# Moving the edge marks and the 0/1 test from the dense layers into the edge layer of a four-layer graph network

## The reference, cut to what matters

```python
x = _layernorm(x + L0(x, adj, nodemask))   # (1+eps) x + adj^T x, two-layer MLP, mask
x = _layernorm(x + L1(x, adj, adj))        # neighbour mean, projection, relu
x = _layernorm(x + L2(x, adj))             # normalised adjacency, projection
x = _layernorm(x + L3(x, adj))

def L3(x, adj):                            # the edge layer
    hi, hj = x @ W1[:H], x @ W1[H:]
    h = relu(hi[:, :, None, :] + hj[:, None, :, :] + b1)   # one row for each pair i, j
    y = layernorm(h @ W2 + b2) * gamma + beta
    return einsum('bij,bijh->bih', adj, y)
```

## Time and profile before

| | us |
|---|---|
| median of 3 runs | 467.81 (466.93 to 469.84) |
| the profiled execution's own time | 470.96 |
| its span, first to last instruction | 469.1 |
| TensorE busy | 439.8 (94%) |
| VectorE busy | 413.1 (88%) |
| ScalarE busy | 386.1 (82%) |
| GpSimd busy | 358.9 (76%) |

### The profile page before, as it was taken

The page is one execution under the profiler, slowest core; times in us unless marked ns, Lnnn a source line. Parts: engine busy times, 40 slices in busy tenths (PEclk is TensorE's granted clock), DMA queues, the critical chain, the costliest instruction groups (busy, mean ns, idle before and its releaser), DMA issues. The chain is left out here.

```text
span 469.1 us, 14149 instructions
## 1 busy us (share of the span) xinstructions
PE 439.8 (94%) x3427; PEld 415.7 (89%) x3427; DVE 413.1 (88%) x1507; ACT 386.1 (82%) x994; POOL 358.9 (76%) x669
## 2 busy tenths in 40 slices
PE   2898989999999999789999999999999999999980
PEld 1798989999999999679999999999999999999980
DVE  4799999999999999937988988898889888989873
ACT  1377979899999899868888888988898889888972
POOL 6279979899999899835776867686768676868655
PEclk9999999999999999989999999999999999999996
DMA  6043335445445652124231313131313131313111
GB/s 216 13 110 93 116 125 166 145 160 166 161 149 156 213 186 82 67 84 149 86 91 52 103 50 101 50 101 50 101 50 101 50 101 50 101 50 96 30 40 48
DMA packets 50796, 47.60 MB, mean 101 GB/s; under 512 B 5441, under 2 KB 42433, under 8 KB 50753
## 3 DMA queue, kind: packets, MB, share of 16 engines
q1 hardware_dynamic: 49744, 45.83, 32.1%
q10 hardware_dynamic: 1008, 1.29, 0.8%
HBM read 28.22 MB, written 18.87 MB: 100 GB/s over the span
## 5 line engine op out<-in xcount | busy, mean ns | idle before, releaser
L1398 PEld LDWEIGHTS bank<-w2c,hE 128*128 128x128 f32 x512 | 67.3, 192 | 2.3
L1398 PE MATMUL bank<-w2c,hE 128*128 128x128 f32 x512 | 67.5, 275 | 0.0
L830 ACT ACTIVATE hE<-bank,front 128x512 f32<-128x512 f32 x64 | 44.3, 692 | 9.0 <-PE bank L1379 8.7
L1110 DVE TENSOR_REDUCE ssum<-sqE 128x4 f32<-128x512 f32 x64 | 43.5, 679 | 7.7 <-ACT sqE L842 6.6
L842 ACT ACTIVATE sqE<-bank 128x512 f32<-128x512 f32 x64 | 38.3, 599 | 13.3 <-PE bank L1398 13.2
L979 DVE BATCH_NORM_STATS2 stats<-t 128x6 f32<-128x128 f32 x192 | 44.6, 274 | 1.7 <-issue 1.5
L1127 DVE TENSOR_TENSOR ym<-bank,wE 128x512 f32<-128x512 f32 x64 | 43.8, 684 | 1.7 <-POOL wE L684 0.4
L659 POOL TENSOR_TENSOR half<-ym 128x512 f32<-128x512 f32 x32 | 40.7, 1272 | 3.1 <-DVE ym L1127 2.6
L646 POOL TENSOR_TENSOR gHl<-gH,gHu 128x512 fp32r<-128x512 f32 x32 | 41.0, 1281 | 1.1 <-issue 1.0
L1396 PE MATMUL bank<-bias,ones_b 128*128 128x512 bf16 x96 | 36.5, 380 | 0.0
L1428 PE MATMUL bank<-yC,ST 128*128 128x128 f32 x256 | 33.9, 275 | 2.8 <-DVE yC L1133 2.8
(11 more groups left out here) (176 smaller groups left out, 1661.2 us busy)
## 6 DMA issues: line engine op xcount, KB each, us to landing
hh_scratch<-hh SPq DMA_DIRECT2D x32, 256.0 KB, 2.3
gH<-hh_scratch SPq DMA_DIRECT2D x32, 256.0 KB, 2.8
A<-adj_groups SPq DMA_DIRECT2D x32, 128.0 KB, 2.1
X<-x_groups SPq DMA_DIRECT2D x32, 128.0 KB, 2.2
res_scratch<-res SPq DMA_DIRECT2D x32, 128.0 KB, 2.1
gRES<-res_scratch SPq DMA_DIRECT2D x32, 128.0 KB, 2.5
out<-y SPq DMA_DIRECT2D x32, 128.0 KB, 1.9
AT<-adjT_groups SPq DMA_DIRECT2D x28, 128.0 KB, 2.4
```

The source lines that it names most:

```text
L830: nc.scalar.activation(hE[g][:, :], HE_ps, ACT.Relu, bias=C["L3_b1"]).then_inc(b[f"hE{g}_ready"], 1)
L1110: nc.vector.tensor_reduce(ssum[q][:, g * ELL:(g + 1) * ELL], sqE[g][:, :, :], AX.X, ALU.add).then_inc(b[f"ssE{g}_ready"], 1)
L1398: last = nc.tensor.matmul(ps[:, i, :], hidden[:, i * P:(i + 1) * P], w2c[:, :], start=False, stop=i == tiles - 1)
```

## The change

The store and reload of the marks go, with their scratch tensor and semaphores. The edge layer loads `AT` again, into a new tile `gAT` (two buffers), and makes the marks on GpSimd and the test on VectorE there. TensorE's `indices` now waits for GpSimd's marks instead of the transfer. The flaw counts come only at the end of the edge layer, so their cast, their matmul (L1327) and the last steps to `most_i` are moved behind the last units (`late_once`). All planned times are new, in both phases: `PERIOD` is 22.4 instead of 24.2, `T3` is another list, and the first edge stages are planned with `EARLY` 15 and `CATCH` 40 instead of 5 and 25, the counts at 201 instead of 217.

```diff
-PERIOD = 24.2
+PERIOD = 22.4
@@ (SP)
-            def load_ot(u, q):
-                sp.dma_start(run(gOT[q][:, :, :]), ot_s[bass.ds(u, 1), :, :].rearrange("o p c -> p (o c)")).then_inc(got_loaded[q], 16)
+            def load_at(u, q):
+                sp.dma_start(run(gAT[q][:, :, :]), at_d[bass.ds(u, 1), :, :].rearrange("o p c -> p (o c)")).then_inc(gat_loaded[q], 16)
...
-            def next_ot(q, u, count):
+            def next_marks(q, u, count):
                 if not isinstance(u, int) or u < UNITS - 2:
-                    sp.wait_ge(b["QT_psum"], count())
-                    load_ot(u + 2, q)
+                    sp.wait_ge(b["ot_ready"], count())
+                    sp.wait_ge(b["flaws_found"], count())
+                    load_at(u + 2, q)
@@ (GpSimd)
-            def mark_edges(k, r, n):
-                pool.wait_ge(at_loaded[k], 16 * r + 16)
-                pool.wait_ge(ot_stored[k], 16 * r + 1)
-                nc.gpsimd.tensor_tensor(ot[k][:, :, :], AT[k][:, :, :], spread_rows(ident[:, :]), ALU.subtract).then_inc(s["ot_ready"], 1)
+            def mark_edges(q, u, count):
+                pool.wait_ge(gat_loaded[q], (u - q) * 8 + 16)
+                wait_past(pool, b["QT_psum"], count(2))
+                nc.gpsimd.tensor_tensor(gOT[q][:, :, :], gAT[q][:, :, :], spread_rows(ident[:, :]), ALU.subtract).then_inc(b["ot_ready"], 1)
@@ (VectorE)
-            def find_flaws(k, r, n):
-                dve.wait_ge(at_loaded[k], 16 * r + 16)
-                wait_past(dve, s["unlike_done"], n - 2)
-                nc.vector.scalar_tensor_tensor(run(unlike[k % 2][:, :, :]), flat(AT[k]), 1.0, flat(AT[k]), ALU.is_equal, ALU.not_equal,
-                                               accum_out=flawed[:, bass.ds(SLOTS * r + k, 1)]).then_inc(s["unlike_done"], 1)
+            def find_flaws(q, u, count):
+                dve.wait_ge(gat_loaded[q], (u - q) * 8 + 16)
+                wait_past(dve, b["flaws_found"], count(2))
+                nc.vector.scalar_tensor_tensor(run(unlike[q][:, :, :]), run(gAT[q][:, :, :]), 1.0, run(gAT[q][:, :, :]), ALU.is_equal, ALU.not_equal,
+                                               accum_out=flawed[:, bass.ds(u, 1)]).then_inc(b["flaws_found"], 1)
...
+            def cast_flaws():
+                dve.wait_ge(b["flaws_found"], UNITS)
+                nc.vector.tensor_copy(flaw[:, B:B + GROUPS], flawed[:, :]).then_inc(flaws_cast, 1)
+
+            def add_flaws():
+                dve.wait_ge(flaws_psum, 1)
                 nc.vector.tensor_reduce(most[0:1, 1:2], flaw_ps[0:1, :], AX.X, ALU.max).then_inc(most_done, 1)
...
+            units(dve, edge_stages, counted=range(-8, 1), late_once={1: cast_flaws, 3: add_flaws})
@@ (TensorE)
+            def count_flaws():
+                pe.wait_ge(flaws_cast, 1)
+                pe.wait_ge(b["TE_ready"], UNITS)
+                pe.wait_ge(b["Qp_ready"], UNITS)
+                nc.tensor.matmul(flaw_ps, ones_b[:, :], flaw[:, :], start=True, stop=True).then_inc(flaws_psum, 1)
...
             def indices(q, u, count):
-                pe.wait_ge(got_loaded[q], (u - q) * 8 + 16)
+                pe.wait_ge(b["ot_ready"], count())
```

More of the change, by code:

```diff
@@ L153, in gnn_stack @@
         most_i = sb("most_i", [1, 1], i32)
+        gAT = [sb(f"gAT{q}", [P, GROUP, P]) for q in K2]
         gOT = [sb(f"gOT{q}", [P, GROUP, P], bf16) for q in K2]
@@ L397, in passage, with units @@
                 call()
-        def units(engine, stages, counted=()):
+        def units(engine, stages, counted=(), late_once={}):
             last = UNITS // 2 - 1
@@ L411, in units @@
                 flow(stages, last + late, constant(last + late), range(late, AGES))
+                if late in late_once:
+                    late_once[late]()
         def every_graph(engine, body):
@@ L496, in store @@
                 sp.dma_start(out_d[bass.ds(u * GROUP, GROUP), :, :].rearrange("g p f -> p g f"), y4[q][:, :, :]).then_inc(out_stored[q], 16)
-            dense_stages = [(24.2, next_a), (25.28, next_x), (25.66, next_at), (26.27, keep(ot, ot_s, "ot_ready", ot_stored)),
-                     (58.51, keep(res, res_s, "res_ready", stored)), (69.62, keep(hh, hh_s, "hh_ready", stored))]
-            edge_stages = [(T3["idx"] + 0.5, next_ot), (max(T3["spl"], T3["hs"]) + 1.5, next_h), (T3["rs"] + 0.8, next_res), (T3["app"] + 1.0, store)]
+            dense_stages = [(22.4, next_a), (24.04, next_x), (28.39, next_at), (51.73, keep(res, res_s, "res_ready", stored)), (55.86, keep(hh, hh_s, "hh_ready", stored))]
+            edge_stages = [(max(T3["mo"], T3["fl"]) + 1.0, next_marks), (max(T3["spl"], T3["hs"]) + 1.5, next_h), (T3["rs"] + 0.8, next_res), (T3["app"] + 0.4, store)]
             rounds(sp, dense_stages)
@@ L1159, in out_rstd @@
                 nc.vector.reciprocal(orstd[q][:, :], ostd[q][:, :]).then_inc(b["orstd_done"], 1)
-            dense_stages = [(5.48, find_flaws), (14.94, sum0), (15.62, stats0), (16.57, var0), (19.4, rstd0), (20.43, apply0), (26.49, degrees), (27.21, sum1a),
-                     (28.48, sum1b), (30.57, stats1), (31.6, inverse_root), (31.93, var1), (32.89, rstd1), (39.51, sum2),
-                     (41.27, stats2), (42.85, var2), (44.78, rstd2)]
-            edge_stages = [(T3["beg"], begin), (T3["T"], slot_edges), (T3["T2"], list_edges), (T3["d0"], sums_ell(0)), (T3["d1"], sums_ell(1)), (T3["dc"], sums_csr),
+            dense_stages = [(11.86, sum0), (13.94, stats0), (15.06, var0), (16.22, rstd0), (18.53, apply0), (24.29, degrees), (25.74, sum1a),
+                     (26.77, sum1b), (27.64, stats1), (30.65, inverse_root), (28.84, var1), (30.51, rstd1), (37.62, sum2),
+                     (38.08, stats2), (39.19, var2), (41.05, rstd2)]
+            edge_stages = [(T3["fl"], find_flaws), (T3["beg"], begin), (T3["T"], slot_edges), (T3["T2"], list_edges), (T3["d0"], sums_ell(0)), (T3["d1"], sums_ell(1)), (T3["dc"], sums_csr),
                       (T3["rec"], invert), (T3["x0"], weigh_ell(0)), (T3["x1"], weigh_ell(1)), (T3["yn"], weigh_csr),
                       (T3["tot"], total), (T3["st"], out_stats), (T3["ag"], out_var), (T3["frec"], out_rstd)]
-            rounds(dve, dense_stages, between={1: center_layer3, 2: split_layer3, 3: edge_tables}, counted=(1, 2, 3))
+            rounds(dve, dense_stages, between={1: center_layer3, 2: split_layer3, 3: edge_tables}, counted=(0, 1, 2, 3))
             passage(dense_stages, edge_stages, once=[(COUNTED, cast_counts), (COUNTED + 1.2, fullest_graph)])
-            units(dve, edge_stages, counted=range(-8, 1))
+            units(dve, edge_stages, counted=range(-8, 1), late_once={1: cast_flaws, 3: add_flaws})
             dve.wait_ge(most_ready, 1)
```

59 lines of the change are left out of this document (25 added, 34 removed), and 9 rows, old and new, of the table T3.

## The result

The changed kernel takes 477.73 us (median of 4 runs, 477.23 to 479.11), the one before 467.98 beside it (466.93 to 469.84). The ratio is 1.0207, with a 95% interval of 1.018 to 1.0234: 2% slower, where 466.5 us was forecast. The profiled execution took 478.21 us with a span of 476.5, so it stands near its median; before, it stood 3 us above. The spans therefore differ by 7.4 us, the medians by 9.7. The kernel before varies with its granted clock: of its executions beside the experiments, those with a mean clock of 0.991 took 466.9 to 468.1 us, those with 0.983 468.2 to 471.0. Its profile was of the second kind (0.983, with the half clock of the earlier trace rows), the changed kernel's has 0.991. That is the likely source of the 2.3 us between the two differences; it was not tested.

The account below looks back on a forecast made before the run. TensorE was taken to bound both dense and edge layers. From the profiled 470.96 us, -4.5 + 4.2 - 1.4 + 0.4 gave 469.7; taking off 3.15 for the profile's distance from the median gave 466.5 us, range 462 to 471.

Parts of the forecast that it names:

- What bounds the kernel: Dense and edge layers both run at TensorE's rate, 5.52 us per group and 7.75 us per unit.
- the turn: Edge layer's rolled loop: at each turn VectorE loses 1.07 us; forecast 0.38 us TensorE wait, 11 turns, +4.2 us.
- Part 1: Dense layers lose tests, marking and store: 4.5 us saved, bounds 2 and 4.7.
- The three delays of the earlier trace: Dense layers: TensorE stalls of 1.77, 1.66 and 0.52 us where VectorE is late; 3.8 us of them recovered.
- Part 2: Edge layer gains marks and tests; VectorE needs 15.7 us per pair against TensorE's 15.49: +4.2 us.
- Rival A: Edge layer: the loop turn's 1.07 us is hidden, TensorE stays the bound: 462.3 us; chance 0.25.
- Rival B: Edge layer: the test collides with GpSimd's split_lower, 0.5 us per unit, +13.2 instead of +4.2: 475.5 us; chance 0.16.
- Full blocking (rival C): Edge layer: the test waits until GpSimd's split_lower ends, some 1.2 us later: 499 us; chance 0.02.
- Part 3: Passage from project1 of group 31 to mlp_ell(0) of unit 1: 26.5 us, -1.4 us, bounds -3.5 and +3.
- Part 4: End of the kernel: flaw cast, matmul and output stages come later, +0.4 us (0 to 2).

Follow-up runs that it names:

- 1: Changed kernel (477.73 us) with VectorE's begin moved from between out_stats and out_var to behind list_edges, right before invert: 470.51 us, ratio 1.0039.
- 2: Changed kernel with GpSimd's add_halves and times_gamma on 2 columns of each group only, VectorE untouched: 469.38 us, ratio 1.0027.
- 6: Changed kernel with begin in its place but in the form that also writes out a sum (accum_out): 468.56 us, ratio 0.9998.
- 7: Kernel of 1 with the test moved to where begin stood, between out_stats and out_var: 469.98 us, ratio 1.0005.
- Experiment 5: Kernel of 1 with the test for 0 and 1 on 2 columns only: 470.67 us, ratio 1.0024.

## Why the prediction was wrong

**What bounds the kernel: right in the main.** TensorE was busy throughout in both phases, and the warning was that VectorE would take over in the edge layer. It did. But 7.75 us per unit is a mean over two distances: outside the loop the units of the kernel before are 7.74 us apart (15.48 per pair), in the loop a pair takes 15.64, so the turn already cost 0.16 us.

**Part 1, right in the sum, not in its terms.** -5.0 us to project1 of group 31 against -4.5 (and outside its bound of 4.7). From 42.51 on the steady distance is 5.53 us. By the second product of the seventh group the start had given 2.2 us (39.08 to 36.88) where 0.7 was forecast. The three delays of the earlier trace rows gave 1.66 of 1.77 us, 0.8 of 1.66 and -0.2 of 0.52 (59.09 to 65.47 and 82.07 to 88.29 are still 0.9 and 0.7 us long), 2.3 us together where 3.8 was forecast. The two misses cancel, and that is luck; the last 0.5 us come in the groups behind.

**Part 2, the step that failed.** The sum said "13.9 us per pair of units, plus 1.07 us ... plus two tests, 0.7: 15.7 us". The 13.9 contains four comparisons at 411 ns, the duration that they have in the old order. The change moves begin to between out_stats and out_var, and the prediction carried the duration along as if it belonged to the instruction. It belonged to the pair of instruction and neighbour. Measured, begin costs 2.06 us more per pair: 13.9 + 0.7 + 2.06 = 16.7 would have been the sum with the turn hidden; the profile has 16.34 us busy (177.93 / 180 x 16.53) and 16.53 us apart. Experiments 1, 2, 6 and 7 each take that wait away in another way and agree: 242.7 to 243.0 us for the edge layer, so 9.5 to 9.8 of the 12.3 us. The rest, 2.5 to 2.8, lies more outside the loop than in it: in the loop pairs are 15.69 us apart in 6 and 15.77 in 1 against 15.64 before, 0.6 to 1.4 us in 11 turns; outside it the first interval grew from 7.32 to 7.84 us and the units stand 0.10 us further apart. TensorE's longer gathers go with that; its cause is argued only.

The term that the prediction did put there, 0.38 us of waiting at each turn, was wrong for this order. With begin moved as in 1, pairs in the loop are 15.77 us apart against 15.69 outside: 0.08 us per turn, half of what the kernel before paid. **Rival A** was right that the turn hides. That the total with begin free (243.0) is close to the forecast's (240.2 + 4.2) is luck: one term absent, another missed.

**Rival B** had the price (475.5) and the mechanism almost: a collision with GpSimd of about 0.5 us, sized by the very row that then moved, begun at 339 to 845 ns. It looked for the collision at the added instruction, which in the loop ends before split_lower begins (334.30 to 334.71 us, split_lower from 334.82). Experiment 5 shows that the test itself costs nothing that can be measured once begin is free; 7 shows that it can collide, but cheaply. One question to the earlier trace rows would have found it: beside what do the 845 ns stand, and where does the new order put begin? The trace of the kernel before answers the first half:
```profile
196.02 1.26 POOL L646 TENSOR_TENSOR gHl<-gH,gHu 128x512 fp32r<-128x512 f32 x1
196.59 1.11 DVE L1089 TENSOR_SCALAR begun<-edge,off 128x256 bf16<-128x256 f32 x2
```
They stand beside split_lower, and the first of the two comparisons ends 0.15 us behind it, as in the changed kernel.

**Full blocking (rival C)** was given 2% on the ground of the test's medians in the dense layers. It is what happens, to begin. At 337.94 the comparisons end only with add_halves, and in the passage one test took 1.35 us beside split_lower. The Trainium skill (SBUF — State Buffer, Who interferes with whom) says more than the prediction used: `tensor_scalar` can take the port pair that VectorE shares with GpSimd, but not in the form that also writes out its accumulator; an instruction with two SBUF inputs contends with GpSimd's reads; `tensor_reduce` doesn't contend. The runs agree on each: 926 ns against 470 in the same place, the test 413 to 631 with add_halves 1280 to 1465, and the reductions at 657 and 678 ns after and before. Evidence from one instruction was used to acquit another.

**Part 3, wrong by 1.5 us.** The two sides cancel. The half clock is gone: project3 takes 1.13 us where it took 2.02. The forecast kept 2 us for it, and took 3.15 us off at the end as the profile's distance from the median, which the changed kernel's profile doesn't have (0.5 us); with the clocks above, the two corrections seem to meet the same loss. TensorE waits instead, in the passage after the change:
```profile
189.73 0.19 PE L1328 MATMUL bank<-cnt,tri 128*128 128x64 bf16 x1 [0.99 <-issue]
...
197.17 0.41 PE L1316 MATMUL bank<-ident,x 128*128 128x128 f32 x2 [0.84 <-ACT hh L781]
...
198.97 1.13 PE L1248 MATMUL bank<-back,x3T 128*128 128x256 f32 x4 [1.18 <-ACT x3T L747]
...
211.16 0.41 PE L1383 MATMUL bank<-TE,gHu 128*128 128x384 f32 x1 [0.74 <-ACT hE L828]
```
The middle two are the dense tail with less edge work between its steps: the cost that the prediction named (slot_edges:0 behind rstd2:31) and didn't give enough. That the fill is the cause was not tested. **Part 4** was +0.7 against +0.4.

## What to carry to other kernels

Before a planned order is changed, list for every VectorE instruction that is moved what GpSimd does at its new place, and the other way round; a duration from the profile holds only beside its old neighbours, and a wide spread of one form (339 to 845 ns) is the sign that it depends on them. A wait of this kind was counted as busy time here, so compare mean durations by line before and after, not waits. Where the instruction can't be placed in a gap, a form of it that doesn't wait may be worth being slower alone: 0.2 us more each here, for 9 us in all.

## What the runs showed of the hardware

- VectorE's comparison of 128x256 f32 against a column, bf16 out: 336 to 352 ns alone, up to 1370 beside GpSimd's `tensor_tensor`; with a sum written out 457 to 482 beside the same instructions, and 0.08 for the read. The loss is not one-sided: GpSimd's weights took 490 ns beside the test and 214 without it.
- With two comparisons in a row each one ended 0.15 us behind a GpSimd instruction of its own, so 0.69 us of work took 1.82.
- A gather's first matmul (128x384, f32) took 418 ns in the median behind runs of eight f32 matmuls of 128 columns, 0.41 us behind the four bf16 matmuls of start_columns, and 339 ns behind place_rows or gather_csr.
- Moving one or two steps of TensorE within its list in this order cost 10 to 15 us (469.98 to 484.85 us, 468.56 to 483.05, 469.98 to 480.32, 468.56 to 479.61), for the larger move with ScalarE waiting 20 us for the gathers from 260 to 440 us; for the smaller one the wait that costs the time isn't known.
